# Cross-attention kernel: one VectorE maximum over two PSUM banks in place of one for each bank

## What is computed

```python
x = layer_norm(hidden, ln1_w, ln1_b)
q, k, v = heads(x @ q_w + q_b), heads(ctx @ k_w + k_b), heads(ctx @ v_w + v_b)
scores = einsum('bhqd,bhkd->bhqk', q, k) * 0.25          # masked, then:
attn = softmax(scores, axis=-1)                          # needs max over the 512 keys
hidden = merge(attn @ v) @ cproj_w + cproj_b + hidden
y = gelu(layer_norm(hidden, ln2_w, ln2_b) @ fc_w + fc_b) @ proj_w + proj_b
h = hidden + y
# second layer: one head, over the same ctx
p = softmax((h @ w_q.T) @ (ctx @ w_k.T).T / 16)
out = h + alpha * ((p @ (ctx @ w_v.T)) @ w_o.T)
```

## Time and profile before

| | us |
|---|---|
| runs, median of 3 | 353.52 |
| lowest and highest | 351.95 and 353.9 |
| span of the profiled execution | 357.1 |
| PE busy | 291.3 (82%) |
| DVE busy | 216.7 (61%) |
| ACT busy | 192.5 (54%) |
| POOL busy | 93.2 (26%) |
| 128 maximum reductions (L1038), DVE busy | 83.8 |
| 128 maximum tiles (L506), PE busy | 49.4 |

### The profile page before, as it was taken

The page is one execution under the profiler, slowest core; times in us unless marked ns, Lnnn a source line. Parts: engine busy times, 40 slices in busy tenths (PEclk is TensorE's granted clock), DMA queues, the critical chain, the costliest instruction groups (busy, mean ns, idle before and its releaser), DMA issues.

```text
span 357.1 us, 5949 instructions
## 1 busy us (share of the span) xinstructions
PE 291.3 (82%) x2053; PEld 199.7 (56%) x2053; DVE 216.7 (61%) x420; ACT 192.5 (54%) x350; POOL 93.2 (26%) x88
## 2 busy tenths in 40 slices
PE   3752869985979898998989999989979898777765
PEld 2540445842216574864756667549565755666554
DVE  5642784457665969766488687664759532537532
ACT  3441364278546487766455857673576864035330
POOL 2152000212100246660022674300126440015200
PEclk9995588789769999999999989999999999878998
DMA  5139991019126205701730181026300000000000
GB/s 185 22 76 181 119 358 42 2 38 127 67 58 77 88 3 100 132 0 39 98 117 1 36 113 72 0 65 68 117 2 1 2 0 2 29 0 2 0 0 31
DMA packets 21485, 22.06 MB, mean 62 GB/s; under 512 B 2388, under 2 KB 18600, under 8 KB 21464
## 3 DMA queue, kind: packets, MB, share of 16 engines
q1 hardware_dynamic: 20024, 18.37, 27.3%
q10 hardware_dynamic: 1440, 3.41, 2.7%
HBM read 11.02 MB, written 1.05 MB: 34 GB/s over the span
## 4 chain that ended last, share of the span: by engine, by line
PE 38%; issue 25%; DVE 12%; ACT 11%; POOL 8%; DMA 3%; SPq 2%; ACTq 0%; DVEq 0%; POOLq 0%
PE post_ps L461 11%; PE post_ps L465 5%; PE om L533 4%; DVE neg_max L1038 4%; PE s L523 4%; PE pre_ps L448 3%; PE s L506 3%; ACT probs L806 2%; ACT q_stack L797 2%; POOL y_l L1339 2%; DMA k_stack<-kp 2%; POOL ln L1279 1%; PE post_ps L584 1%; ACT y_h L820 1%; PE post_ps L665 1%
## 5 line engine op out<-in xcount | busy, mean ns | idle before, releaser
L1038 DVE TENSOR_REDUCE neg_max<-s 128x1 f32<-128x512 f32 x128 | 83.8, 683 | 33.1 <-PE s L506 32.8
L806 ACT ACTIVATE probs<-s 128x512 f32<-128x512 f32 x128 | 75.6, 599 | 43.9 <-PE s L523 43.0
L506 PE MATMUL s<-k_stack,q_stack 97*128 97x512 bf16 x128 | 49.4, 423 | 18.6 <-DMA k_stack<-kp 14.1
L523 PE MATMUL s<-q_stack,k_stack 109*128 109x256 bf16 x256 | 51.6, 286 | 0.5 <-ACT q_stack L797 0.3
L533 PE MATMUL om<-probs,vals 128*17 128x256 f32 x512 | 42.9, 410 | 5.4 <-ACT q_stack L797 2.7
L523 PEld LDWEIGHTS s<-q_stack,k_stack 109*128 109x128 bf16 x256 | 17.1, 100 | 37.0 <-issue 22.5
L1279 POOL TENSOR_TENSOR ln<-ln,minus_half 128x2 f32<-128x2 f32 x8 | 5.6, 702 | 95.9 <-DVE ln L1002 95.9
L506 PEld LDWEIGHTS s<-k_stack,q_stack 97*128 97x128 bf16 x128 | 13.0, 103 | 29.1 <-DVE neg_max L1038 12.8
L1064 DVE TENSOR_TENSOR y_l<-post_ps,y_h 128x512 fp32r<-128x512 f32 x16 | 11.0, 691 | 29.9 <-ACT y_h L820 29.9
L797 ACT ACTIVATE q_stack<-om 13x1024 bf16<-13x1024 bf16 x16 | 16.3, 1016 | 14.2 <-PE om L513 13.9
L533 PEld LDWEIGHTS om<-probs,vals 128*17 128x17 f32 x512 | 9.0, 96 | 23.5 <-issue 15.7
(11 more groups left out here) (226 smaller groups left out, 676.4 us busy)
## 6 DMA issues: line engine op xcount, KB each, us to landing
k_stack<-kp SPq DMA_DIRECT2D x48, 128.0 KB
q_stack<-qp SPq DMA_DIRECT2D x48, 64.0 KB
cx<-in_ctx_dram SPq DMA_DIRECT2D x5, 512.0 KB, 6.2
pcx<-in_ctx_dram ACTq DMA_DIRECT2D x3, 512.0 KB, 3.6
xz<-in_x_dram SPq DMA_DIRECT2D x5, 256.0 KB, 5.2
raw_late<-in_L_xattn_fc_w_dram SPq DMA_DIRECT2D x1, 1024.0 KB, 12.3
raw_late<-in_L_xattn_proj_w_dram SPq DMA_DIRECT2D x1, 1024.0 KB, 12.1
h<-in_x_dram ACTq DMA_DIRECT2D x3, 256.0 KB, 2.5
```

Of the source, the lines that this page charges most:

```text
L506: pe.matmul(s1[:, s % 2, :], q_stack[0:ROW_MAX, hd, chunk(t)], k_stack[0:ROW_MAX, hd, :], start=True, stop=True).then_inc(s1_full, 1)
L523: mm = pe.matmul(s2[:, s % 2, i * LQ:(i + 1) * LQ], k_stack[:, hd, chunk(k)], q_stack[:, hd, :], start=True, stop=True)
L806: act.activation(probs[:, g % 2, s // 2, k:k + 2, :], s2[:, s % 2, :].rearrange("p (k n) -> p k n", k=2), ACT.Exp).then_inc(s2_free, 1)
L1038: dve.tensor_reduce(neg_max[:, g % 2, s % 2, s // 2:s // 2 + 1], s1[:, s % 2, :], AX.X, ALU.max, negate=True).then_inc(s1_free, 1)
```

## The change

`take_max` reduces both banks of `s1` with one instruction: the input is 128 x 2 x 512, the output two columns of `neg_max`, for the two query tiles of a head. It is called only for odd tiles (1, 3, 5, 7), waits on `s1_full` until the odd tile of the pair is there, and then adds 2 to `s1_free` at its end. PE's side, its order and its wait, is not edited. Since tiles 4 to 7 stand in slots of their own, the reduction of tile 4 moves from DVE's slot 2 to slot 3, and that of tile 6 from slot 4 to slot 5.

```diff
             def take_max(b, g, s):
                 dve.wait_ge(s1_full, NS * b + SLOTS * g + s + 1)
-                dve.tensor_reduce(neg_max[:, g % 2, s % 2, s // 2:s // 2 + 1], s1[:, s % 2, :], AX.X, ALU.max,
-                                  negate=True).then_inc(s1_free, 1)
+                dve.tensor_reduce(neg_max[:, g % 2, :, s // 2], s1[:], AX.X, ALU.max, negate=True).then_inc(s1_free, TQ)
...
-                for s in range(SLOTS):
+                for s in range(1, SLOTS, TQ):
                     take_max(0, 0, s)
...
                     for i in MAX_TILES[s]:
-                        take_max(nb, ng, i)
+                        if i % TQ == TQ - 1:
+                            take_max(nb, ng, i)
```

## The result

The new kernel takes 372.66 us (median of four runs, 371.39 to 375.63), the kernel before in the same comparison 352.74 (351.89 to 353.9): a ratio of 1.055, 95% interval 1.0496 to 1.0604. A ratio leaves out runs that are over 1.5% longer than the fastest of the same kernel; a median holds them. The forecast was 367.9 with a range from 359.5 to 372.5: the direction is as forecast, the median lies 4.8 us above the forecast and 0.2 us above the upper end of the range, which is less than the spread of the four runs.

A forecast was written before the change was run, and what follows sets the result against it. PE, busy 82% of the span, was taken to bound the kernel; stalls summed to 15.1 us, less 0.6 gave 14.5 us, 4.1% of the profiled 357.1 us, so 353.52 x 1.041 = 367.9 us; range 359.5 to 372.5 us.

The forecast's parts named there:

- The rival of two passes at 1.37 us: Every pair reduction runs as two passes of 683 ns: 3.7 us more, 371.6 us; chance 0.13 together with a lower clock.
- The walk: Whole timeline, pair of tiles by pair: added delay before PE may write the next even tile, 15.1 us in all.
- The estimates for the full periods: Periods 115 to 183 and 183 to 251 us: 1.6 + 0.5 + 0.6 = 2.7 us lost in each, 5.4 us together.
- The stalls at tiles 2 and 6 of group 3: Full periods, DVE behind: tile 2 released 0.54 us later, tile 6 0.9 us late, 1.1 with what is carried.
- the wait of the transposes at the split: Full periods, group 3: the transpose already waits for the split, and the last reduction ends 0.54 us later.
- The cover of batch 0 group 3: PE's 4.02 us wait for the stacking copies hides two stalls of 0.6 us, so 0 is lost there.
- Tile 6 behind the normalisation: Batch 3 group 2: tile 6 must wait for the pair reduced after the normalisation, about 1.4 us lost.
- Batch 0 group 1: Three even-tile intervals 0.76 us longer each, last pair about 0.3 us later: 2.6 us together.
- Batch 1 groups 0 and 1: Tile 6 stalls twice by 0.6 us: 1.2 us; the 1.50 us wait for the split moves with it.
- The handovers: Between PE's matmuls and DVE's reduction, both ways: 0.1 us for both, counted in every pair.
- The clock: More PE idling holds the clock down; one more half-clock slice costs 3 to 5 us; chance 0.13 together with two passes.
- The 0.6 us that DVE's relief was to give back: Some 12 pairs of group 3 where PE waits for DVE: 0.05 us saved on each, 0.6 us off the sum.

The follow-up runs named there:

- The wait alone: Kernel before, with PE filling an even tile only when both tiles before it are reduced, reductions still single: 364.86 us, ratio 1.0289.
- four banks in the prologue: New kernel with batch 0's first group alternating its pairs between the maximum tiles' and the exponential tiles' banks: 369.29 us, ratio 1.0414 to the kernel before.
- the second trace of before: Kernel before, unchanged, profiled again: 353.26 us, ratio 0.9997; this profiled execution spans 351.3 us.
- The fillers: New kernel with three unread matmuls added after each of the prologue's first three pairs: 371.18 us, ratio 1.0496 to the kernel before.
- the kernel whose prologue had no added stalls: New kernel with single reductions in the first group of batch 0 only: 368.31 us, ratio 1.0402 to the kernel before.
- ten runs: Kernel before with pair reductions and PE's tiles 4 and 6 one slot later, in batches 1 to 3 only: 355.56 us, ratio 0.9968.

## Why the prediction was right, and where its size was off

**Order of reading.** The prediction held that the fewer instructions are worth almost nothing and that PE's unedited wait changes its meaning when `s1_free` moves in steps of 2. Both came out. The wait alone costs 2.9%; four banks in the prologue make the loss of that group vanish.

**The price of a pair.** 1.22 us was taken from an instruction on other memory with as many elements; it measured 1221 ns. The rival of two passes at 1.37 us is out.

**The walk.** The estimates for the full periods, 2.7 and 2.7, met 2.7 and 3.1, in part by luck. Counted from a group's first tile to the next group's, the first period lost 0.3, 0.5, 1.2 and 0.7 us in groups 2, 3, 0 and 1, where the sum had 0, 1.6, 0.5 and 0.6. The stalls at tiles 2 and 6 of group 3 are there (0.80 us each), but those at tiles 3 and 4 of before (0.21 and 0.77) shrank to nothing that shows and 0.51, and the wait of the transposes at the split, which the forecast had 0.5 longer, is gone. The cover of batch 0 group 3 held: PE still waits for the stacking copies after it, 2.25 us instead of 4.02, and nothing is lost there.

```profile
95.16 0.61 PE L506 MATMUL s<-k_stack,q_stack 97*128 97x512 bf16 x2 [2.25 <-DMA k_stack<-kp]
```

**Batch 3 group 2.** Tile 6 behind the normalisation, 1.4 us in the forecast. The rows after:

```profile
270.43 0.74 DVE L1008 TENSOR_SCALAR z<-h,ln 128x256 f32<-128x256 f32 x2 [0.81 <-POOL ln L1279]
271.08 1.22 DVE L1038 TENSOR_REDUCE neg_max<-s 128x2 f32<-128x1024 f32 x1
...
272.36 0.39 PE L506 MATMUL s<-k_stack,q_stack 97*128 97x512 bf16 x1 [2.50 <-DVE neg_max L1038]
...
272.58 0.60 PE L584 MATMUL post_ps<-ident,z 128*128 128x128 f32 x4
```

The mechanism is the one forecast: PE waits 2.50 us at the tile, the transposes of the normalised rows follow at once. The distance from the normalisation to these transposes grew from 260.10 - 259.31 = 0.79 to 272.58 - 270.43 = 2.15, by 1.36 us.

**Where the size was off.** The sum was 15.1 us before its correction; from the first tile on 18.4 were lost, and the timed runs say 19 to 20. The sum counted stalls alone; PE's idle time grew by 14.1 us, and the rest is busy time at a lower clock. Three terms were too small.
- *Batch 0 group 1*: 2.6 against 4.3. The step "0.76 for each of three intervals" took the one interval shown, between tiles 2 and 4, for all. Between tiles 4 and 6 lies an exponential tile too, and the clock was at half. The rows after:

```profile
48.98 0.61 PE L506 MATMUL s<-k_stack,q_stack 97*128 97x512 bf16 x1 [1.17 <-DVE neg_max L1038]
...
50.55 1.23 DVE L1038 TENSOR_REDUCE neg_max<-s 128x2 f32<-128x1024 f32 x1 [1.62 <-PE s L506]
...
51.84 0.61 PE L506 MATMUL s<-k_stack,q_stack 97*128 97x512 bf16 x1 [0.96 <-DVE neg_max L1038]
```

  Tile 4 to tile 6 is 2.86 us here; in the second trace of before it is 1.20. That one interval costs 1.66 us. From tile 6 to the transposes another 1.1 us is lost, where the forecast had 0.3.
- *Batch 1 groups 0 and 1*: 1.2 against 2.4, with the clock at 0.75 instead of 0.82 of full in that stretch, and a tile 2 that waits 0.45 us, which the walk had left out. Of the two stalls forecast at tile 6 only that of group 1 appears (0.51 us). PE's busy time grew by 2.3 us in this stage, so nearly all of the loss is the same matmuls taking longer.
- *The handovers*: 0.1 us in the forecast, 0.11 + 0.05 = 0.16 measured in the prologue. That is 0.06 for each stall, an estimate of 1 to 2 us for PE's 24 waits.

The clock was named as a rival with 371 to 373 us, which is where the result fell. It came true in part: the forecast's mechanism carries most of the loss, and a lower clock, mostly in batches 0 and 1, adds to it. How much the clock alone is worth is not settled. The fillers gained 1.6 us in a trace. The two traces of the kernel before give an estimate: up to the last transpose the first had 16.6 us more at half clock and took 6.1 us longer. The kernel after has 21.2 us more there than the second; PE's busy time grew by 7.7 of the 19.7 us lost. Whether the stalls brought the clock down everywhere, or only moved the work to other places in time, no run separates. The 0.6 us that DVE's relief was to give back can't be seen. The tail's gain of 1.4 us, where no maxima are taken, goes with its clock.

**The span that the forecast was scaled by** was of an execution 5.8 us longer than the second one. It did no harm to the sum, since its stalls sat at the same instructions, but it hid stretches of half clock that the second trace doesn't have, and with them what the change would do to the clock.

## What to carry to other kernels

Before merging two instructions that each free a buffer, ask what is left for the producer while the merged one runs: with two buffers and one instruction over both, two engines that overlapped take turns, and here that cost 5.5% to save 5.7 us of busy time on an engine that was 61% busy. The cost stands only where the producer comes back before the merged instruction is done; where a slot of other work lay between, in batches 1 to 3, pairs cost nothing that ten runs could tell. A semaphore that now moves in steps of 2 changes the meaning of every wait on it, edited or not.

## What the runs showed of the hardware

- A maximum over 2 x 512 float32 in two PSUM banks takes 1221 ns and one over 512 takes 683, but in a row they come 1.2 us apart and 0.6 us apart: the rate is the same, and the 0.15 us that the records suggest as saved for each merged pair isn't there.
- Stalls and a lower clock came together: after 8 us in which PE was busy 3.08 in place of 6.97, it was granted 0.62 of full clock over 14 us, where group 1 had 1.00 before. With fillers, 7.22 of 8 us busy, it was 0.74. But the clock also fell at 44.6 us in the kernel whose prologue had no added stalls.
- Two executions of the same kernel differed by 5.8 us, most of it in three stretches at half clock.
